# A spare scatter ahead of Pool's first one, the mask's transfer ahead of k2's high part, and the first unit's passes waiting by four blocks

## The reference

```python
mask = jnp.full((N, N), -jnp.inf, dtype=dtype)
mask = mask.at[src, dst].set(w[edge_type - 1])
q = x @ wq.T + bq
q2 = (q @ wiq.T + biq).reshape(N, H, D).transpose(1, 0, 2)
scores = jnp.einsum('hnd,hmd->hnm', q2, k2) * scale + mask[None]
attn = jax.nn.softmax(scores, axis=-1)
```

## Time and profile before

| | us |
|---|---|
| median of three runs | 820.29 |
| lowest, highest | 819.74, 823.03 |
| the profiled execution | 820.27 |
| its span, first to last instruction | 818.2 |
| TensorE busy in it | 810.5 |
| DVE, Pool, ACT busy | 482.8, 461.2, 374.9 |

### The profile page before, as it was taken

The page is one execution under the profiler, slowest core; times in us unless marked ns, Lnnn a source line. Parts: engine busy times, 40 slices in busy tenths (PEclk is TensorE's granted clock), DMA queues, the critical chain, the costliest instruction groups (busy, mean ns, idle before and its releaser), DMA issues.

```text
span 818.2 us, 14141 instructions
## 1 busy us (share of the span) xinstructions
PE 810.5 (99%) x5016; PEld 649.4 (79%) x5016; DVE 482.8 (59%) x1105; ACT 374.9 (46%) x614; POOL 461.2 (56%) x297
## 2 busy tenths in 40 slices
PE   8999999999999999999999999999999999999998
PEld 8999998888888779898488588588488488488476
DVE  7898864444443256998545545645645645646545
ACT  5433336566556343244634535535535535535531
POOL 4786784333443426557665664674664664664652
PEclk9999999999999999999999999999999999999999
DMA  8676653532222329533697697697596697697684
GB/s 297 195 221 185 191 167 133 174 108 77 77 77 104 104 80 343 194 115 138 137 268 258 145 276 246 143 272 265 129 268 246 149 265 254 143 256 262 151 226 164
DMA packets 66177, 153.38 MB, mean 187 GB/s; under 512 B 9392, under 2 KB 22320, under 8 KB 66128
## 3 DMA queue, kind: packets, MB, share of 16 engines
q1 hardware_dynamic: 51904, 120.93, 42.4%
q0 software_dynamic: 10944, 24.82, 16.7%
q10 hardware_dynamic: 3280, 6.98, 3.1%
HBM read 122.06 MB, written 37.97 MB: 196 GB/s over the span
## 4 chain that ended last, share of the span: by engine, by line
PE 96%; DVE 1%; DMA 1%; ACT 1%; issue 0%; POOL 0%; SPq 0%; DVEq 0%; ACTq 0%
PE bank L1594 26%; PE bank L1596 25%; PE bank L1595 25%; PE bank L1925 12%; PE bank L1648 2%; PE bank L1737 2%; PE bank L1641 2%; PE bank L1709 2%; DMA x<-in_x 1%; DMA mask<-mask_scratch 1%; DVE stats L939 0%; ACT scratch L733 0%; PE bank L1683 0%; POOL rstd L500 0%; DVE x L1133 0%
## 5 line engine op out<-in xcount | busy, mean ns | idle before, releaser
L568 POOL TENSOR_TENSOR w_lo<-w_raw,w_hi 128x1024 fp32r<-128x1024 f32 x67 | 165.8, 2476 | 136.3 <-ACT w_hi L820 129.5
L1594 PE MATMUL bank<-w_hi,hT_hi 128*128 128x512 f32 x480 | 189.8, 395 | 0.9 <-DVE hT_lo L958 0.8
L1596 PE MATMUL bank<-w_hi,hT_lo 128*128 128x512 f32 x480 | 187.5, 391 | 0.0
L1595 PE MATMUL bank<-w_lo,hT_hi 128*128 128x512 f32 x480 | 187.2, 390 | 0.0
L508 POOL TENSOR_TENSOR w_lo<-w_raw,w_hi 128x1024 fp32r<-128x1024 f32 x39 | 94.7, 2430 | 100.4 <-ACT w_hi L651 75.9
L820 ACT ACTIVATE w_hi<-w_raw 128x1024 fp32r<-128x1024 f32 x84 | 88.8, 1057 | 128.1 <-PE bank L1596 90.3
L1594 PE MATMUL bank<-hT_hi,w_hi 128*128 128x384 f32 x320 | 107.9, 337 | 0.0
L1595 PE MATMUL bank<-hT_lo,w_hi 128*128 128x384 f32 x320 | 107.0, 334 | 0.0
L1596 PE MATMUL bank<-hT_hi,w_lo 128*128 128x384 f32 x320 | 106.9, 334 | 0.0
L1594 PEld LDWEIGHTS bank<-w_hi,hT_hi 128*128 128x128 f32 x480 | 90.5, 189 | 20.3 <-issue 1.8
L1596 PEld LDWEIGHTS bank<-w_hi,hT_lo 128*128 128x128 f32 x480 | 90.1, 188 | 19.2
(11 more groups left out here) (226 smaller groups left out, 1272.2 us busy)
## 6 DMA issues: line engine op xcount, KB each, us to landing
w_raw<-in_units SPq DMA_DIRECT2D x145, 512.0 KB
late<-in_units SPq DMA_DIRECT2D x56, 512.0 KB
scratch<-slots_scratch SPq DMA_DIRECT2D x7, 512.0 KB, 7.3
scratch<-in_src_row ACTq DMA_DIRECT2D x8, 384.0 KB
scratch<-in_dst_row ACTq DMA_DIRECT2D x8, 384.0 KB
sums_scratch<-zeros SPq DMA_DIRECT2D x1, 1536.0 KB, 8.2
sums_scratch<-x SPq DMA_DIRECT2D x1, 1536.0 KB, 10.5
x<-sums_scratch SPq DMA_DIRECT2D x3, 512.0 KB, 4.7
```

The source lines that it names most:

```text
L568: pool.tensor_tensor(w_lo[:, s, :], w_raw[:, s, :], w_hi[:, s, :].bitcast(fp32), ALU.subtract).then_inc(lo_ready[s], 1)
L1594: pe.matmul(dst, a_hi, b_hi, start=first, stop=False)
L1595: pe.matmul(dst, a_hi, b_lo, start=False, stop=False)
L1596: return pe.matmul(dst, a_lo, b_hi, start=False, stop=last)
```

## The change

Three edits. Pool gets one more indirect scatter, of 128 words (the constant -0.5) into the first 128 words of slots_scratch, right after w_lo of unit 0, and waits for its landing ahead of the zeros; its index list row_i is made earlier for that. ACT's waits for `bo_added` and the 48 scatters and the issue of the mask's transfer stand ahead of k2_hi and w_hi of unit 28. On TensorE one warm-up product is left of three ahead of unit 0, and the first and the third pass wait by four blocks.

```diff
--- before.py
+++ after.py
@@ -277,6 +277,7 @@
         bank += [psum(f"bank{i}", 512) for i in range(5, 8)]
         keys = two_banks[:, 0:PIECE * P]
         slots_dram = nc.dram_tensor("slots_scratch", (SLOT_TILES, P), fp32).ap()
+        slot_words = slots_dram.rearrange("a (d k) -> (a d) k", k=1)
         sums_dram = nc.dram_tensor("sums_scratch", (2 * N, D), fp32).ap()
         mask_dram = nc.dram_tensor("mask_scratch", (N * N, 1), fp32).ap()
         mask_blocks = mask_dram.rearrange("(t p b n) k -> p t b (n k)", t=NT, p=P, b=NT)
@@ -289,6 +290,7 @@
         x_landed = [sem(f"x_landed{t}") for t in range(NT)]
         consts_landed, bo_landed = sem("consts_landed"), sem("bo_landed")
         pool_consts, pool_step, dve_consts = sem("pool_consts"), sem("pool_step"), sem("dve_consts")
+        spare_landed = sem("spare_landed")
         var_ready, rstd_ready, shift_ready, normed_ready = (sem("var_ready"), sem("rstd_ready"),
                                                                  sem("shift_ready"), sem("normed_ready"))
         normed_T, hT_hi_done, hT_lo_done = sem("normed_T"), sem("hT_hi_done"), sem("hT_lo_done")
@@ -522,13 +524,19 @@
                                pattern=[[1, PIECE * P]], channel_multiplier=-1).then_inc(pool_consts, 1)
             for e in range(FE):
                 pool.memset(desc[:, e:e + 1], float(FE - e)).then_inc(pool_consts, 1)
+            pool.iota(row_i[:], pattern=[[1, 1]], base=0, channel_multiplier=1).then_inc(ffn_consts, 1)
             pool.wait_ge(pool_consts, 1)
             rstds_of(0, 0, NT)
             pool.wait_ge(last_normed, NT - 1)
             make_lo(0, 0)
+            pool.wait_ge(ffn_consts, 1)
+            pool.indirect_dma_start(out=slot_words, out_offset=bass.IndirectOffsetOnAxis(ap=row_i[:], axis=0),
+                                    in_=minus_half[:], in_offset=None, bounds_check=SLOT_TILES * P - 1,
+                                    oob_is_err=False).then_inc(spare_landed, 16)
             pool.wait_ge(picks_made, 4)
             make_lo(2, 2)
             make_lo(3, 0)
+            pool.wait_ge(spare_landed, 16)
             pool.memset(zeros[:], 0.0).then_inc(zeros_ready, 1)
             pool.tensor_tensor(picked[:, 0:2, :], picked[:, 0:2, :], picked[:, 2:4, :], ALU.add).then_inc(pool_step, 1)
             pool.wait_ge(pool_step, 4)
@@ -547,7 +555,6 @@
             pool.memset(ahead, 1.0).then_inc(pool_step, 1)
             pool.memset(ones, 1.0).then_inc(ffn_consts, 1)
             pool.iota(count_i[:], pattern=[[1, P]], base=0, channel_multiplier=0).then_inc(ffn_consts, 1)
-            pool.iota(row_i[:], pattern=[[1, 1]], base=0, channel_multiplier=1).then_inc(ffn_consts, 1)
             for c in range(6):
                 pool.memset(block_of[:, c:c + 1], float(c - 8)).then_inc(ffn_consts, 1)
             pool.wait_ge(pool_step, 6)
@@ -739,11 +746,11 @@
 
             q2_hi_of(0, bias[:, 3, 0:1])
             hi_fixed(U_PAIR + 3)
-            k2_hi_of(0, bias[:, 4, 0:1], 0)
-            hi_fixed(U_PAIR + 4)
             act.wait_ge(bo_added, PAIRS)
             act.wait_ge(edges_landed, 16 * CHUNKS)
             act.dma_start(mask8[:], mask_dram.rearrange("(t p n) k -> p t (n k)", t=NT, p=P)).then_inc(mask_landed, 16)
+            k2_hi_of(0, bias[:, 4, 0:1], 0)
+            hi_fixed(U_PAIR + 4)
             exp_of(0, 0)
             exp_of(0, 1)
             with act.Fori(1, PAIRS) as j:
@@ -1675,17 +1682,19 @@
             keep_warm(6)
             first_normed_turns(1)
             first_normed_turns(2)
-            keep_warm(3)
+            keep_warm(1)
 
             pe.wait_ge(hi_ready, 1)
-            pe.wait_ge(hT_hi_done, LN_STEPS)
             for k in range(KT):
+                if k % 4 == 0:
+                    pe.wait_ge(hT_hi_done, LN_STEPS - 1 + k // 4)
                 pe.matmul(bank[0][:, 0:N], w_hi[:, 0, k * P:(k + 1) * P], hT_hi[:, k, :], start=k == 0, stop=False)
             unit_ready(0, 0)
             for k in range(KT):
                 pe.matmul(bank[0][:, 0:N], w_lo[:, 0, k * P:(k + 1) * P], hT_hi[:, k, :], start=False, stop=False)
-            pe.wait_ge(hT_lo_done, LN_STEPS)
             for k in range(KT):
+                if k % 4 == 0:
+                    pe.wait_ge(hT_lo_done, LN_STEPS - 1 + k // 4)
                 last = pe.matmul(bank[0][:, 0:N], w_hi[:, 0, k * P:(k + 1) * P], hT_lo[:, k, :], start=False,
                                  stop=k == KT - 1)
             last.then_inc(unit_used, 1)
```

## The result

The median before is 820.03 us (six runs, 819.68 to 823.03), after the change 825.00 us (six runs, 823.26 to 825.58). The ratio is 1.005 with a 95% interval of 1.0037 to 1.0063: 0.5% slower, where 0.9 us less was forecast. The profiled execution took 825.6 us.

A forecast was written before the change was run, and what follows sets the result against it. TensorE, busy 810.5 of 818.2 us, was taken as the bound, with a little over 1 us of its idle time at stake. The mask's 0.8 and the start's 0.1 off 820.27 gave 819.4 us, range 818.4 to 821.2.

The forecast's parts named there:

- hides it whole: Pool's idle time from 14.45 to 19.71 us would cover the added scatter's 0.97 to 1.62 us.
- that wait is free: Pool's wait for the added scatter's landing, asked for at 24.5 us, ten us after issue, would cost nothing.
- The bound for its landing, 3.6 us: Later scatters land within 3.6 us (109.25 to the next start at 112.86), taken for the added one too.
- Its three signs of being wrong: Mask issue beyond 122.1 us, added scatter reaching 19.7, or a new TensorE stop between 133 and 144.
- The first use: Pool's first real scatter at 28.44 us pays 0.1 to 0.75 us; removing it gains 0.1 on unit 6's w_lo.
- Rival 4: Added scatter outlasts Pool's 5.26 us gap and delays unit 2: 820.3 us, or 821.1 by code load; chance 0.03.
- The mask: Before pair 0's turns: mask issued at 121.9 instead of 122.72 us, ahead of k_hi, gaining 0.8 us.
- The 0.4 us from the last bytes to the semaphore: Estimate that the last scatter before the mask, its traffic ending at 121.4 us, signals at 121.8.
- Rivals 1 and 3: Last scatter before the mask lands at 122.1 to 122.7 (820.0 us, chance 0.17) or 123.5 (821.1 us, chance 0.06).
- Unit 0: First pass 0.5 us sooner, but Pool's w_lo lets unit 2 start only 0.07 sooner, at 22.15; 0.1 us taken.
- The sum: 0.8 us for the mask's transfer plus 0.1 for the start, 0.9 us off 820.27: 819.4 us predicted.
- no case of "slower": Late scatter landing before the mask, 821.1 us, chance 0.06; code load, 821.1; slower beyond 0.5%, chance 0.02.

The follow-up runs named there:

- the later spare scatter: Kernel before plus the scatter of 128 adjacent words, issued after w_lo of unit 3 near 24.5 us: 821.15 us against 820.11, ratio 1.0017.
- the plain transfer: Kernel before plus one plain SP transfer of the same 128 adjacent words behind the first reloaded weight tile, no scatter: 826.81 us beside 821.28.
- the scatter in turn 3: Kernel before plus the scatter of 128 adjacent words behind the six scatters of turn 3, near 73 us: 826.50 us, one execution.

## Why the prediction was wrong

- **The spare scatter: the step that failed is that Pool's idle 5.26 us "hides it whole".** On Pool all went as written: 1.21 us in the gap, which ended by DVE's picks, and "that wait is free" held too, since the zeros started without a stop behind w_lo. I costed the scatter on the engine that issues it and gave the effect of its 128 writes on other transfers nothing, since they are half a kilobyte. Measured, it is about 5 us: 4.8 us with the spare scatter alone, 0.1 with the same words 4 KB apart. The bound for its landing, 3.6 us, came from scatters into a mask table of 576 KB; this one wrote neighbours, and landed in 9.0. It held up the weight tiles and the diagonal behind it, and the diagonal is what Pool's first real scatter waits for. The prediction had that dependence (27.5 us), and that unit 6 hangs on it, and didn't ask what the new transfer does to it. Its three signs of being wrong watched the mask's issue, Pool's gap and TensorE from 133 to 144 us, and no landing.
- **The first use.** Expected 0.1 us on w_lo of unit 6, ends 0 and 0.7; the run with the words apart shows 0. The reading that most of the 2.79 us were a landing was right: with the diagonal later, they became 5.75.
- **Rival 4** looked for the loss in Pool's time, from 5.26 us on. It was 1.21 us at this place in every run with 128 words, harmful or not. The Trainium skill's 6 us of code load ("GPSIMD Engine Reference", "Instruction dispatch") don't show in any scatter here. In after the very first one ran its 1.21 us after 0.19 us of idle.
- **A stop's second price.** No case had the clock. In after the stop was followed by a stretch at half clock that cost 1.6 us more.
- **The mask: right.** The issue was put 0.8 us sooner, and came 0.85 sooner against k_hi; and the stop went whole: 1.0 us instead of 0.8. The transfer took 3.8 to 3.9 us instead of 4.43, but kernels in which it wasn't moved have 3.8 to 4.5, so that isn't the move's doing. The 0.4 us from the last bytes to the semaphore stood on no row; the traces of the moved issue show 0.4 to 0.5 (last bytes by 121.25, issue at 121.71 in the change without its spare scatter). Rivals 1 and 3, the late landing, didn't come.
- **Unit 0: right.** 0.56 us sooner for 0.5, unit 2 at 22.11 for 22.15, unit 6 with 0.16 us less for 0.1.
- **The sum** of 0.9 us less lies within both intervals of the change without its spare scatter (1.0 less to 0.6 more, and 2.1 to 0.6 less). The range, 818.4 to 821.2, missed 825.0 by that one term, and no case of "slower" held more than 0.9 us.

## What to carry to other kernels

A transfer of a few hundred bytes is not free because it is small: ask where its elements land, what is queued behind it, and who waits for that. A dummy or warm-up write should spread its words: at this place 32 bytes apart and more did no harm (one execution for each of 32, 64 and 512 bytes, ten for 4 KB). And before removing a "first-use" gap, look for the landing that the engine waits for there.

## What the runs showed of the hardware

128 single words written side by side in memory slowed the transfers of this core for some 6 to 8 us, by GpSimd's queue as by SyncE's: traffic mostly under 50 GB/s (under 100 in the later spare scatter) where 200 to 400 ran, and landings of 9.0 to 10.8 us for the words themselves; by the landings the harm is about half at 8 bytes and gone at 32. Which part does it, the write path of the DMA engines or the memory, stays open: no run tells them apart. The traces show that the engines were busy meanwhile, with ten times as long for a packet of q1. The Trainium skill, "DMA: Bandwidth & Descriptors", "Specifications", says that transfers under 512 bytes are done by reading and rewriting. That would fit neighbours that hold each other up, but the words 64 bytes apart are as small and cost nothing, so the size alone isn't it.

The granted clock around a stop of TensorE, the stops by its weight loads. With a stop of 2.4 us (the words 8 bytes apart) it stayed at 2.4 GHz. With 3.4 us (the spare scatter alone) it fell to its lower level 0.3 us before the stop's end and stayed there for 3.4 us, from 42.8 to 46.2 us. With 3.8 us (after) it stayed up through the stop and for 1.4 us of work, and then fell for 3.4 us, from 45.2 to 48.6. With 4.3 and 4.5 us (the plain transfer, and the scatter in turn 3) it fell 1.6 and 2.1 us before the stop's end, and stayed down for 6.8 us. So the length of the stop alone doesn't say when it falls. The last of these, its stop from 88.6 to 93.06, in stretches with their granted clock:

```profile
89.00:91.00 2.00, 0.00 (x0) 0.00 (x0) 1.06 (x2) 1.54 (x2) 1.68 (x3) 0.98 0.01 0
91.00:97.50 6.50, 4.44 (x14) 4.44 (x15) 6.18 (x7) 0.00 (x0) 5.73 (x4) 0.50 0.50 186
97.50:100.00 2.50, 2.50 (x15) 2.50 (x14) 0.00 (x0) 0.17 (x1) 1.89 (x3) 0.95 0.84 332
```

So the work behind the longest stop, from 93.1 to 97.5 us, is 14 matmuls, where the next 2.5 us have 15.
